# A causal mask moved from VectorE into the score accumulation of an attention kernel, with a new order of projections at the turn between batches

## The reference

```
q, k, v = layernorm(x) @ w.T + b                    # 16 heads of 64, for each of 2 batches
scores  = q k^T / 8; scores = where(key > query, -inf, scores)   # causal
attn    = (softmax(scores) v) @ wo.T + bo
x       = x + layernorm(attn)
x       = x + layernorm(ffn(layernorm(x)))          # gated choice of one of 8 low-rank experts
```

## Time and profile before

| | us |
|---|---|
| median of three runs | 2574.5 (2570.42 to 2576.23) |
| profiled execution, its own time | 2570.42 |
| its span in the trace | 2568.4 |
| first `times_v` to last (pairs 0 to 15) | 117.2 to 2091.1 |
| work after the attention | about 477 |

### The profile page before, as it was taken

How to read it: one execution, slowest core, us unless ns; L and a number is a source line. 1 busy time by engine, 2 the same in 40 slices (tenths; PEclk the granted TensorE clock), 3 DMA queues, 4 the chain that set the end, 5 groups by cost and what they waited for, 6 DMA issues and landing times. The chain is left out here.

```text
span 2568.4 us, 72133 instructions
## 1 busy us (share of the span) xinstructions
PE 2317.3 (90%) x28626; PEld 1453.9 (57%) x28626; DVE 1793.0 (70%) x4218; ACT 1712.2 (67%) x2451; POOL 1837.3 (72%) x1551
## 2 busy tenths in 40 slices
PE   4899999999999998889999999999996559999995
PEld 2556666565757655556575757566664335444442
DVE  8577877677777655556666766666665637888886
ACT  3477777777877766567777777777777834444443
POOL 4477888788888867678888888888887734555553
PEclk9999999999999999999999999999998779999997
DMA  9599999999999999989999999999999866666663
GB/s 236 124 186 181 200 195 191 195 195 186 199 190 198 177 186 188 193 154 182 175 180 179 171 189 175 187 164 182 173 166 198 172 142 142 151 158 160 153 149 89
DMA packets 1433646, 450.17 MB, mean 175 GB/s; under 512 B 1410240, under 2 KB 1411536, under 8 KB 1433312
## 3 DMA queue, kind: packets, MB, share of 16 engines
q1 hardware_dynamic: 1433312, 445.57, 95.2%
HBM read 67.95 MB, written 41.94 MB: 43 GB/s over the span
## 5 line engine op out<-in xcount | busy, mean ns | idle before, releaser
L815 POOL TENSOR_TENSOR hl<-probs,hl 128x1024 f16<-128x1024 f32 (+7 forms) x768 | 1231.8, 1615 | 395.7 <-ACT hl L696 394.2
L690 ACT ACTIVATE probs<-s_ps,exp_bias 128x1024 f32<-128x1024 f32 (+7 forms) x768 | 655.7, 854 | 410.3 <-DVE exp_bias L541 406.3
L538 DVE TENSOR_REDUCE neg_max<-s_ps 128x1 f32<-128x1024 f32 (+7 forms) x768 | 694.6, 904 | 66.5 <-PE s_ps L396 66.1
L696 ACT ACTIVATE hl<-probs 128x1024 f16<-128x1024 f32 (+7 forms) x768 | 620.5, 808 | 48.1 <-DMA pt<-hl 24.1
L414 PE MATMUL o_ps<-v,pt 128*128 128x65 f16 x4352 | 453.6, 194 | 84.5 <-DMA pt<-hl 75.0
L396 PE MATMUL s_ps<-nat 64*128 64x512 f16 (+3 forms) x3840 | 434.6, 355 | 69.3 <-ACT probs L690 64.9
L414 PEld LDWEIGHTS o_ps<-v,pt 128*128 128x128 f16 x4352 | 404.5, 97 | 136.3 <-DMA pt<-hl 64.2
L415 PE MATMUL o_ps<-v,pt 128*128 128x65 f16 x4352 | 453.5, 195 | 0.0
L416 PE MATMUL o_ps<-v,pt 128*128 128x65 f16 x4352 | 451.5, 193 | 0.0
L443 PE MATMUL u_ps<-arena,w 128*128 128x512 f16 x1008 | 389.7, 387 | 40.2 <-DMA arena<-hl 35.2
L415 PEld LDWEIGHTS o_ps<-v,pt 128*128 128x128 f16 x4352 | 404.3, 98 | 27.0
(11 more groups left out here) (148 smaller groups left out, 3791.8 us busy)
## 6 DMA issues: line engine op xcount, KB each, us to landing
w_raw<-in_w_pairs SPq DMA_DIRECT2D x48, 576.0 KB, 4.7
o_scratch<-o_hl SPq DMA_DIRECT2D x128, 128.0 KB, 2.5
out<-result SPq DMA_DIRECT2D x32, 512.0 KB, 3.6
x_in<-in_x SPq DMA_DIRECT2D x27, 512.0 KB, 4.6
pt<-hl SPq DMA_TRANSPOSE x768, 4.6
nat<-in_x SPq DMA_DIRECT2D x16, 512.0 KB, 4.5
xn_scratch<-xn SPq DMA_DIRECT2D x16, 512.0 KB, 4.7
xn<-in_x SPq DMA_DIRECT2D x11, 512.0 KB, 4.0
```

The source lines that it names most:

```text
L538: nc.vector.tensor_reduce(neg_max[:, r, acc, h:h + 1], s_ps[n % S_RING][:, 0:nb * P], AX_X, ALU.max, negate=True).then_inc(max_done, 1)
L690: nc.scalar.activation(probs[n % P_RING][:, 0:nb * P], s_ps[n % S_RING][:, 0:nb * P], ACT.Exp, bias=exp_bias[:, r, acc, h:h + 1], scale=SO ...
L696: nc.scalar.activation(hl[n % HL_RING][:, 0:nb * P], probs[n % P_RING][:, 0:nb * P], ACT.Copy).then_inc(p_hi_done, 1)
L815: nc.gpsimd.tensor_tensor(hl[n % HL_RING][:, w:2 * w], probs[n % P_RING][:, 0:w], hi, ALU.subtract).then_inc(p_lo_done, 1)
```

## The change

The mask is no longer added by VectorE. Behind the last three products of a diagonal step, TensorE adds it in the accumulation of the same PSUM block, as unit matrix times mask. Since each head's matmul has only 64 rows of the array, the 128 rows of the mask come in two parts, so there are 2 x 2 more matmuls of 64 rows and 128 columns in a step, with bfloat16 operands (the range of -1e30 needs it). The mask instructions of VectorE and the semaphore between mask and maximum are gone. The unit rows are one more small load at the start, and TensorE waits for it before its first projection.

The schedule around the projections changes too. In pairs 6 and 7 the units have a new order, with q of chunk 0 second instead of fifth. In kinds "mid", "pre" and "turn" the q weights are split at step 1 instead of 4; in "pre" and "turn" k goes from step 20 to 18 and v from 23 to 22. The turn's transposes are eight and eight, and start two steps earlier.

```diff
-         "turn": [("k", 0), ("v", 0), ("k", 1), ("v", 1), ("q", 0), ("q", 1), ("k", 3), ("v", 3), ("q", 3), ("k", 2),
+         "turn": [("k", 0), ("q", 0), ("v", 0), ("k", 1), ("q", 1), ("v", 1), ("k", 3), ("q", 3), ("k", 2), ("v", 3),
                   ("v", 2), ("q", 2)],
...
-SPLITS = {kind: {4: "q", last_step(kind, "k") + 1: "k",
-                 max(last_step(kind, "k") + 4, last_step(kind, "v") + 1): "v"} for kind in ("mid", "pre", "turn")}
+SPLITS = {kind: {1: "q", last_step(kind, "k") + 1: "k", last_step(kind, "v") + 1: "v"} for kind in ("mid", "pre", "turn")}
...
-TURN_STEPS = {"pre": {10 + 2 * i: i for i in range(7)}, "turn": {2 * i: 7 + i for i in range(9)}}
+TURN_STEPS = {"pre": {8 + 2 * i: i for i in range(8)}, "turn": {2 * i: 8 + i for i in range(8)}}
...
+        unit_rows = sb("unit_rows", [P, 2, P], BF16)
-        mask = sb("mask", [P, P], F32)
+        mask = sb("mask", [P, 2, P], BF16)
...
+                    diagonal = end == nb * P and k0 + nb == t + 1
                     for q, k in ((q_lo, k_hi), (q_hi, k_lo), (q_hi, k_hi)):
                         for h in range(2):
                             mm = nc.tensor.matmul(s_ps[(n + h) % S_RING][:, at:end], qk[HEADS[h], q, rows],
-                                                  qk[HEADS[h], k, keys], start=(q == q_lo), stop=(q == q_hi and k == k_hi))
+                                                  qk[HEADS[h], k, keys], start=(q == q_lo),
+                                                  stop=(q == q_hi and k == k_hi and not diagonal))
+                    if diagonal:
+                        for part in range(2):
+                            for h in range(2):
+                                mm = nc.tensor.matmul(s_ps[(n + h) % S_RING][:, end - P:end], unit_rows[HEADS[h], part, :],
+                                                      mask[HEADS[h], part, :], start=False, stop=(part == 1))
...
             def row_max(p, i):
                 r, (t, k0, nb, acc) = i // PER_ROUND, steps_of(p)[i]
-                diagonal = k0 + nb == t + 1
-                masked = 2 * (QT * p + sum(k0 + nb == t + 1 for t, k0, nb, acc in steps_of(p)[:i]))
-                dve.wait_ge(s_done, NTASK * p + 2 * i + 2)
-                if diagonal:
-                    for h in range(2):
-                        last = s_ps[(NTASK * p + 2 * i + h) % S_RING][:, (nb - 1) * P:nb * P]
-                        nc.vector.tensor_tensor(last, last, mask[:], ALU.add).then_inc(mask_done, 1)
                 for h in range(2):
                     n = NTASK * p + 2 * i + h
-                    if diagonal:
-                        dve.wait_ge(mask_done, masked + h + 1)
+                    dve.wait_ge(s_done, NTASK * p + 2 * i + 2)
```

More of the change, by code:

```diff
@@ L10 @@
 F16 = mybir.dt.float16
+BF16 = mybir.dt.bfloat16
 AX_X = mybir.AxisListType.X
@@ L124, in units_ending, with attend_phase @@
     return [i // STEPS_PER_UNIT] if UNITS[kind] and i >= 0 and i % STEPS_PER_UNIT == STEPS_PER_UNIT - 1 else []
-def attend_phase(nc, x, w_pairs, mask_in, xn_scratch, o_scratch, arena, fin):
+def attend_phase(nc, x, w_pairs, unit_in, mask_in, xn_scratch, o_scratch, arena, fin):
     with ExitStack() as ctx:
@@ L198, in attend_phase @@
         s_done = sem("s_done")
-        mask_done = sem("mask_done")
         max_done = sem("max_done")
@@ L249, in weight_at, with next_split @@
             return 3 * p + {"k": 1, "v": 2, "q": 3}[m]
[L251 to L255, removed]
+        def next_split(p, kind, i):
+            m = SPLITS[kind].get(i)
             target = p + 1 if m == "q" or kind == "first" and i == 1 else p + 2
@@ L330, in body @@
                         transpose_probs(*step)
-                    split = next_split(p, i - 1)
+                    split = next_split(p, kind, i - 1)
                     if split:
@@ L364, in _ @@
             sp.dma_start(fin["ident"][:], fin["ident_in"]).then_inc(consts_loaded, 16)
+            sp.dma_start(unit_rows[:], unit_in).then_inc(consts_loaded, 16)
             sp.dma_start(mask[:], mask_in).then_inc(consts_loaded, 16)
@@ L459, in body @@
                         times_v(p, i, h)
+            pe.wait_ge(consts_loaded, 48)
             for u in range(LAST_CHUNK):
@@ L652, in _ @@
                 unit_full(0, u)
-            dve.wait_ge(consts_loaded, 32)
             for i in range(LAG):
@@ L752, in body @@
                             unit_high(p + 1, u)
-                    split = next_split(p, i)
+                    split = next_split(p, kind, i)
                     if split:
@@ L1432, in _, with attention_ffn @@
             steps(step)
-def attention_ffn(nc, x, w_pairs, w_o, b_o, ffn_in, ffn_probe, ffn_mix, center, slope, ident, mask, own,
+def attention_ffn(nc, x, w_pairs, w_o, b_o, ffn_in, ffn_probe, ffn_mix, center, slope, ident, unit_rows, mask, own,
                   rank, out):
@@ L1440, in attention_ffn @@
         fin = finish_inputs(nc, ctx, x, o_scratch, w_o, b_o, ident, ffn_in, ffn_probe, ffn_mix, own, rank, center, slope)
-        attend_phase(nc, x, w_pairs, mask, xn_scratch, o_scratch, fin["arena"], fin)
+        attend_phase(nc, x, w_pairs, unit_rows, mask, xn_scratch, o_scratch, fin["arena"], fin)
         finish_phase(nc, fin, out)
@@ L1447 @@
            L0_ffn_lora_degen, L0_ffn_bias_w, L0_ffn_debias_w):
+    import ml_dtypes
     import numpy as np
@@ L1465 @@
                              np.arange(N_EXP)])
+    by_half = lambda m: np.tile(m.reshape(2, HD, P).transpose(1, 0, 2), (2, 1, 1)).astype(ml_dtypes.bfloat16)
     arrays = {
@@ L1477 @@
         "ident": np.eye(P, dtype=np.float32),
-        "mask": np.where(np.arange(P)[None, :] > np.arange(P)[:, None], -1e30, 0.0).astype(np.float32),
+        "unit_rows": by_half(np.eye(P)),
+        "mask": by_half(np.where(np.arange(P)[None, :] > np.arange(P)[:, None], -1e30, 0.0)),
         "own": (np.arange(2 * N_EXP)[:, None] == expert[None, :]).astype(np.float32),
```

## The result

The changed kernel takes 2615.0 us (median of 4 runs, 2601.6 to 2622.9) against 2574.0 for the kernel before on the same chip: a ratio of 1.0155, 95% interval 1.0111 to 1.0200, some 40 us slower. The forecast was 2582 us, with a range up to 2597. The sign was right, the size five times too small, and the time lies outside the range. The profiled execution took 2608.13 us with a span of 2606.2, so 37.8 us of the difference can be looked for in the two traces.

What follows compares the result with a forecast made beforehand. TensorE was taken to bound pairs 9 to 14 almost alone. Pairs 0 to 5 -0.3, 6 to 8 +0.9, 9 to 14 +5.6, pair 15 -1.6, turn +2.8: +7.4 us, so 2582 us around the median; range 2566 to 2597.

Steps and rivals of the forecast that it cites:

- The mask's price on TensorE: On 256 diagonal steps, the added mask matmuls cost TensorE 0.11 us a step, 28.2 us at the full clock.
- The other q splits: In the "mid" pairs, q split at ScalarE's step 1 instead of 4: zero, between -4 and +4 us over twelve pairs.
- three signs of being wrong: Pairs 9 to 14 not longer, scores' exponential waits in pairs 0 to 5 vanishing, or the turn moving over 10 us.
- Pairs 0 to 5 and 9 to 14, the return from waits: Exponential waits there shrink 0.29 us each, DMA waits some 0.15; net with the mask's cost -0.3 and +5.6 us.
- The turn: Pairs 6 to 8: q waits of 2.8 and 4.8 us, less 4.8 from v; +2.8 us, between -5 and +10.
- VectorE's busy time: Sign in the profile: VectorE's busy time lower by the mask's 126 us, with little of it in the span.
- Faster by the score buffers: Scores' waits for the previous exponential, everywhere: nearly all recovered, -18 us, so 2556; half of it 2565; chance 0.19.
- Nothing measurable: Extra TensorE time comes out of its idle time; pairs 0 to 8 gain, 9 to 14 lose; 2574 to 2577 us; chance 0.22.
- Heads don't overlap: Mask matmuls of two heads don't overlap, or operand switches cost: 0.22 us or more a step, 2605 us; chance 0.09.

Runs made afterwards that it cites:

- e1: The kernel before with only the mask moved to TensorE, unit orders, splits and x tiles as before: 2593.9 us, ratio 1.0078.
- e3: The changed kernel with the q split of the "mid" pairs back at step 4: 2590.8 us, ratio 1.0059 to the kernel before.
- e5: The kernel before with only the q split of the "mid" pairs moved from step 4 to 1: 2596.7 us, ratio 1.0090.
- after: The changed kernel, with the whole change made to the kernel before: 2615.0 us, ratio 1.0155.
- e10: The kernel before with the mask on TensorE, and VectorE's weight split put ahead of its evacuation of the finished unit: 2593.4 us, ratio 1.0099.
- e6: The kernel before with the new order, splits and x tiles of "pre" and "turn" only, "mid" pairs untouched: 2571.3 us, ratio 0.9995.
- e4: The changed kernel with SyncE's four stores moved from step 2 to 5, q split left at 1: 2592.2 us, ratio 1.0070 to the kernel before.
- e7: The kernel before with only the mask moved to TensorE and every mask matmul issued twice: 2591.6 us, ratio 1.0076.

## Why the prediction was wrong, step by step

- **The mask's price on TensorE** held. 28.2 us for 256 steps was forecast; pairs 9 to 14 show 9.3 us for 96 steps in e1, 0.097 each. The matmuls of the two heads overlap as those of the scores do, and the bfloat16 operand costs nothing that shows.
- **The step that failed: "The other q splits", taken as zero, between -4 and +4 us.** By e3 it is 24 us of the 41, and by e5 on the kernel before 23. The step weighed one ScalarE instruction against two exponentials. The split also frees `w_raw`, so it moves a DMA on SyncE: 576 KB beside 4 x 128 KB, ahead of the eight-block transposes. The prediction followed that queue for the turn, in the earlier trace rows, and not for the twelve "mid" pairs. It counted ScalarE's part of the moved step and not what the step releases. With both ahead of them the transposes of step 6 are issued so late that nothing is left over (in pairs 1 to 13 of after the second one landed at most 0.07 us before its `times_v` began), and an instruction packet makes a wait of 2.4 us or more out of that, with a stretch at 1.2 GHz behind it. None of the prediction's three signs of being wrong looks at these pairs' splits, and none came true.
- **Pairs 0 to 5 and 9 to 14, the return from waits**: 0.29 us for each wait for an exponential and 0.15 for each DMA wait. This treated each wait as one that is shortened. In e1 the number of waits in pairs 9 to 14 fell from 24 to 11, but their sum stayed (11.6 us): the shift let three of VectorE's v splits start just behind GpSimd's work and take 3.18 us instead of 1.21, and the DMA waits that were left became longer. In e10 the v splits are short again and nothing is gained, so the 3.18 us is not the whole reason, and what keeps the sum up stays open. Forecast for the mask without the turn +4.6 us, measured 20. Of the 17.6 us in the profiled spans, 9.6 lie in pairs 9 to 14 (9.3 busy and no return). The rest is spread: 3.0 us in pairs 0 to 5, 1.3 in 6 to 8, 3.2 in pair 15, where -1.6 was forecast, and 0.6 outside.
- **The turn**: +2.8 forecast, -1 measured (e6, within its interval of zero). Waits of 2.8 and 4.8 us for q were forecast, 2.86 and 6.01 came; the two waits behind the v splits are gone, and that for the last x tile stayed at 3.67. That SyncE catches up in such a stall stood in the range and not in the sum: DMA waits in pairs 6 to 8 fell from 24.3 us to 20.4 in e6 and 16.2 in after. ScalarE's wait for v is gone, as forecast; it now waits for q, 3.05 us in pair 7 and 1.49 in pair 8. The latter was costed at nothing, or some 2 us if its cover failed; in after TensorE waits 2.13 us for the exponential behind it (at 1155.16), in e6 nothing above 0.8. (In the order of before shown above, row 273 is the load of the q weights, not of k: `SPLITS` has v at step 23 there, and q follows v.)
- **The clock** had no term outside the turn. It costs 13.7 of the 37.8 us in the profiled execution. It is no cause of its own: three of the four stretches at 1.2 GHz in pairs 9 to 14 stand behind the step-6 waits, the fourth behind one of 2.81 us at step 1 of pair 11, and all four are gone in e4.
- **VectorE's busy time** was to fall by 126 us and fell by 84.7 (1793.0 to 1708.3). 9.9 us went back into longer weight splits (group of line 512: 91.6 us, before 81.7), and the mask's records overlapped others, as the two of the earlier trace rows do.
- **The rivals.** "Faster by the score buffers" had the mechanism half right: the waits for exponentials in pairs 0 to 5 did fall, from 18.5 to 12.1 us in e1, and to 1.3 in pairs 9 to 14 of after. In pairs 0 to 5 the waits of both kinds fell by 7.6 us, but TensorE was 11.6 us busier; in pairs 9 to 14 of after the waits for DMAs rose by more. "Nothing measurable" came closest in e7, where a second mask went into idle time, and not in e1. "Heads don't overlap" would have needed some 20 us of TensorE's time in pairs 9 to 14 in e1; it was 9.3.

Why the collision waits in pairs 9 to 14 show with the mask on TensorE (after) and hardly without it (e5), the traces answer in part: in pairs 9, 11 and 13 of after an instruction packet fell into the transfer, in pairs 9 to 13 of e5 none did. What stays open is what moves these packets against the transposes from kernel to kernel; no run holds them fixed. Parts overlap as well: mask 20, early q split 24 and the turn nothing make 44 where 41 were measured, within the spread of the runs of after (2601.6 to 2622.9). And the stretches at 1.2 GHz in pairs 0 to 5 differ from kernel to kernel (3 to 24 us) in a way that I can't derive from the edits.

## What to carry to other kernels

When a step is moved, list what it releases as well as what it occupies: a buffer it frees starts a load, that load takes a place in a DMA queue, and what stands behind it there may be what the bounding engine waits for next. Idle time of the bounding engine is not a reserve against which an addition can be booked before it is known which chain makes it: here, in pairs 9 to 14, a first 9 us of added work took none of 12 us, and a second 10 us took 9. When waits of one kind come in some repetitions and not in others, look in those places for traffic that the program didn't issue, here the packets of instructions. Try a new place for work and the order around it together, since the mask cost 20 us in the old order and about 8 in one where loads, stores and splits stood apart.

## What the runs showed of the hardware

- A VectorE instruction on data in SBUF (scalar_tensor_tensor, 128x1024, f32 to f16) took 1.21 us when it began 0.33 us before GpSimd's (1475.95 against 1476.28), and 3.18 when it began 0.03 us behind it in e1. GpSimd's took 2.87 us in the first case and 2.13 in the second. Begun 0.23 us behind, as the k splits of before, VectorE's took 2.98. In these pairs the one that starts second is stretched; only with starts within 0.03 us could it go either way (in after, at 1492.38 and 1492.36, VectorE's took 1.22 and GpSimd's 3.23). The maximum of 1024 columns on PSUM took 1.21 or 1.22 in the rows beside them. The Trainium skill (GPSIMD Engine Reference, Specifications) says that GpSimd shares its SBUF interfaces with VectorE, with contention where VectorE's instruction has two SBUF inputs, as this one has; the trace agrees.
- In pairs 9 to 14 of after a stretch of 3.4 us at 1.2 GHz lay behind each of the four waits of 2.45 to 2.82 us, in a stream that was otherwise busy (it began between 0.6 us before the wait's end and 0.9 behind it), and in e3 behind one of 1.92; none lay behind the waits of 1.4 us in e4. In pairs 0 to 5 some waits of that length had none (2.43 us in e1, 2.87 in e3). At half speed a stretch adds 1.7 us.
- In pair 11 of after the load of 576 KB took SyncE 0.57 us to issue and the four stores 2.49, and the next two transposes 3.56 and 1.82 us; where the load was elsewhere (e3) they took 2.17 and 2.33. In the "mid" pairs up to 13 the first of the two took 3.4 to 4.4 us in after and 1.5 to 3.5 in e3.
- A DMA transpose of 128x2048 float16 from SBUF to SBUF (the second of step 6) landed 4.3 to 4.4 us after its issue in pairs 1, 2, 4, 7, 8, 10 and 12 of after, and 6.0 to 6.3 us after it in pairs 3, 5, 6, 9, 11 and 13, where a packet of 16 KB of instructions had begun 4.1 to 4.3 us behind the issue. For some 1.4 us of this the DMA engines together moved 20 GB/s or less. Over all transposes of eight blocks in pairs 1 to 14 of after, the 66 with such a packet 3 to 5 us behind the issue landed after 6.1 us in the median, the other 214 after 4.9. That the packet is the cause is not tested by a run.
